# VectorE makes the low halves of two contexts before the masking passes of the same step, instead of after them

## What is computed

```python
def gnn(h, Wq, bq, Wk, bk, Wv, bv, Wf, bf, mask):
    q, k, v = heads(h @ Wq + bq), heads(h @ Wk + bk), heads(h @ Wv + bv)
    scores = einsum('bhqd,bhkd->bhqk', q, k) / sqrt(64)
    probs = softmax(scores + where(mask, 0, -9e15), axis=-1)
    ctx = einsum('bhqk,bhkd->bhqd', probs, v)
    return merge_heads(ctx) @ Wf + bf

for layer in (0, 1):
    h = maximum(layernorm(x), 0)
    x = x + gnn(h, *weights[layer], adj)
```

## Time and profile before

| | |
|---|---|
| median of three runs | 1950.31 us |
| profiled execution | 1948.68 us, span 1946.9 us |
| PE matmuls busy | 1838.3 us, 94% of the span |
| DVE busy | 1640.3 us, 84% |
| ACT busy | 1549.7 us, 80% |
| POOL busy | 1485.0 us, 76% |
| DMA | 61.5% of 16 engines, 187 GB/s |
| granted TensorE clock, mean | 0.997 |

### The profile page before, as it was taken

How to read it: one execution, slowest core, us unless ns; L and a number is a source line. 1 busy time by engine, 2 the same in 40 slices (tenths; PEclk the granted TensorE clock), 3 DMA queues, 4 the chain that set the end, 5 groups by cost and what they waited for, 6 DMA issues and landing times.

```text
span 1946.9 us, 54319 instructions
## 1 busy us (share of the span) xinstructions
PE 1838.3 (94%) x17210; PEld 1040.0 (53%) x17210; DVE 1640.3 (84%) x5555; ACT 1549.7 (80%) x4789; POOL 1485.0 (76%) x1777
## 2 busy tenths in 40 slices
PE   8899999999999999999999999999999999999998
PEld 3455555555555555555555555555555555555554
DVE  7988888888888888888888888888888888888876
ACT  5768878888887888788788888888887888788874
POOL 4568887887788788878878887887888788778762
PEclk8999999999999999999999999999999999999999
DMA  6556666666666666666666666666666666665555
GB/s 198 166 151 186 196 190 185 183 193 192 195 184 190 187 189 196 196 185 181 194 191 195 190 186 181 189 197 194 183 190 186 193 191 191 182 185 174 177 166 187
DMA packets 439942, 363.32 MB, mean 187 GB/s; under 512 B 207700, under 2 KB 406888, under 8 KB 439656
## 3 DMA queue, kind: packets, MB, share of 16 engines
q1 hardware_dynamic: 439656, 359.86, 61.5%
HBM read 184.30 MB, written 175.37 MB: 185 GB/s over the span
## 4 chain that ended last, share of the span: by engine, by line
PE 56%; DVE 33%; issue 7%; POOL 1%; DMA 1%; SPq 1%; ACT 1%; DVEq 0%; POOLq 0%; ACTq 0%
PE ps_shared L665 13%; PE ps_shared L667 12%; PE ps_shared L666 12%; DVE probs L1289 11%; PE ps_qk L665 6%; PE ps_qk L667 6%; PE ps_qk L666 6%; DVE p_blocks L1230 6%; DVE ct_lo L1263 6%; DVE h_blocks L1230 3%; DVE stats L1225 3%; DVE qk_lo L1269 1%; DVE x_tile L1300 1%; SPq L367 1%; DMA p_dram<-p_blocks 1%
## 5 line engine op out<-in xcount | busy, mean ns | idle before, releaser
L540 POOL TENSOR_TENSOR probs<-probs,row_rcp 128x768 f32<-128x768 f32 x252 | 371.3, 1473 | 308.9 <-DVE row_rcp L1254 308.9
L986 ACT ACTIVATE probs<-probs,row_min 128x128 f32<-128x128 f32 x1512 | 582.8, 390 | 2.5 <-DVE row_min L1289 2.5
L1289 DVE CUSTOM_DVE_ANT_0 probs<-ps_scores,mask,minus_scale 128x128 f32<-128x128 f32 x1512 | 430.9, 348 | 1.7 <-issue 1.2
L552 POOL TENSOR_TENSOR p_half<-p_moved,p_half 128x768 f16<-128x768 f32 x236 | 387.4, 1642 | 2.0 <-ACT p_half L961 2.0
L1300 DVE SCALAR_TENSOR_TENSOR x_tile<-ps_shared,out_scale,x_tile 128x384 f32<-128x384 f32 x256 | 157.9, 617 | 229.6 <-PE ps_shared L667 224.5
L948 ACT ACTIVATE v<-ps_shared 128x384 f16<-128x384 f32 x236 | 115.6, 490 | 262.2 <-PE ps_shared L667 262.2
L665 PE MATMUL ps_shared<-wv_hi,ht_hi 128*128 128x384 f16 x756 | 246.8, 326 | 81.4 <-DVE ct_lo L1263 81.4
L1269 DVE SCALAR_TENSOR_TENSOR qk_lo<-ps_qk,qk_bias,qk_hi 128x512 f16<-128x512 f32 x384 | 276.0, 745 | 39.8 <-ACT qk_hi L969 39.5
L986 ACT ACTIVATION_READ_ACCUMULATOR probs<-probs,row_min 128x1 f32 x1512 | 287.0, 190 | 0.0
L969 ACT ACTIVATE qk_hi<-ps_qk,qk_bias 128x512 f16<-128x512 f32 x384 | 257.6, 671 | 14.7 <-PE ps_qk L667 14.6
L536 POOL TENSOR_TENSOR x_tile<-x_tile,out_bias 128x384 f32<-128x384 f32 x256 | 257.5, 1007 | 1.1 <-DVE out_bias L1213 1.1
(11 more groups left out here) (144 smaller groups left out, 3967.3 us busy)
## 6 DMA issues: line engine op xcount, KB each, us to landing
p_dram<-p_blocks SPq DMA_DIRECT2D x256, 384.0 KB, 2.4
p_moved<-p_dram SPq DMA_DIRECT2D x1024, 96.0 KB, 2.4
h_dram<-h_blocks SPq DMA_DIRECT2D x252, 192.0 KB, 2.5
h_moved<-h_dram SPq DMA_DIRECT2D x1008, 48.0 KB, 2.0
x_tile<-in_x SPq DMA_DIRECT2D x128, 192.0 KB, 2.8
out_x<-x_tile SPq DMA_DIRECT2D x128, 192.0 KB, 2.5
adj_u<-in_adj SPq DMA_DIRECT2D x64, 64.0 KB, 2.5
wv_raw<-in_L_gnn_Wv SPq DMA_DIRECT2D x2, 576.0 KB, 4.7
```

What stands on the lines that cost most here:

```text
L540: nc.gpsimd.tensor_tensor(probs_of(t, i), probs_of(t, i), row_rcp[i % 2][:, :].rearrange("p (a o) -> p a o", o=1) .to_broadcast([P, HEADS, ...
L552: nc.gpsimd.tensor_tensor(p_part(i, 1), p_moved[i % 2][:, :, :].rearrange("p a n -> p (a n)"), p_part(i, 0), ALU.subtract).then_inc(p_set, 1)
L986: ins = nc.scalar.activation(tile[:, s, :], tile[:, s, :], ACT.Exp, bias=row_min[i % 2][:, s:s + 1], scale=-1.0, accum_out=row_sum[i % 2][ ...
L1289: ins = nc.vector.tensor_tensor_reduce(tile[:, s, :], score_bank(i, s // PAIRS)[:, (s % PAIRS) * P:(s % PAIRS + 1) * P], mask[b][:, i, :], ...
```

## The change

In `slot` of the DVE program, the calls of `ctx_lo` for the two contexts of an even step stand before `mask_and_min(t, i)` instead of after it. In odd steps there is no `ctx_lo`, so nothing moves there. No instruction is added or removed, and no other engine's list changes. The semaphore waits in `ctx_lo` (for `ct_hi_set`) and in `mask_and_min` (for `scored`, `mask_set`, `p_blocked`) go with their calls.

```diff
                     if exists(eu):
                         invert_sums(eu, ei)
-                    if exists(t):
-                        mask_and_min(t, i)
                     for cu, ci in pair_at(t, i):
                         if exists(cu):
                             ctx_lo(cu, ci)
+                    if exists(t):
+                        mask_and_min(t, i)
                     if t == 1:
                         weights_lo(1, CAST_ORDER[i])
```

## The result

The changed kernel takes 1856.04 us, the median of four runs (1854.17 to 1859.71), against 1949.99 us for the kernel before in the same job. The ratio is 0.952, with a 95% interval of 0.9504 to 0.9536. The forecast was 1852.3 us in a range of 1847 to 1868. In the profiled executions the span went from 1946.9 to 1852.4 us, 94.5 us less.

The account below looks back on a forecast made before the run. PE, nearly always busy, was taken to be held up by waits for DVE's ct_lo. Removing about 119 stalls, 98 us in all, from 1950.3 us gave 1852.3 us, range 1848 to 1859, widened to 1847 to 1868.

Parts of the forecast that it names:

- The bound: PE standing still for ct_lo of DVE before project_v in even steps: 83.8 us in 122 waits, some 0.8 us each.
- The move of the low halves: On DVE in even steps, ct_lo comes 1.63 us earlier, covering PE's stall with 0.84 or 0.80 us to spare.
- The masks 0.9 us later, and the wait in front of them: On DVE in even steps, masks end about 0.94 us later and stand behind ct_lo's wait for ct_hi: cost nothing.
- The sum: About 119 stalls lost 100 us: 96 us regular, 4 us from longer ones; 98 us taken as gain.
- DMA has no place on this path: On the path after the even-step stall goes, transfers were claimed to play no part; no size given.
- PE's busy time stays at 1838: Profile sign if right: PE's busy time unchanged at 1838 us, its share rising to about 99%.
- No change: Rival: DVE, not PE, sets the pace, so time stays at 1950 us; chance 0.03.
- The partial rival: Rival: DVE late by r beyond 0.45 us before the output, i = 2; r = 0.5 gives 1882 us; chance 0.08.
- The slower rival: Rival: late ct_hi makes DVE wait in front of the masks, delaying PE; up to 2065 us; chance 0.04.
- its decision point: Delay of the second ct_hi against DVE beyond which a pair of steps gets longer than before: 2.03 us.

Follow-up runs that it names:

- the shortened PE: PE leaves out two matmuls in each even step: 1952.71 us in the old order, 1830.44 us in the new order.
- the half change: The kernel before, with the low halves ahead of the masks only in even steps with i = 0: 1902.67 us.
- the runs with three and four passes ahead: Changed kernel with the two low halves behind the third or fourth of the six masking passes: 1858.54 us and 1886.08 us.
- the old order with the fifth DMA: Kernel before, with SP moving each h_moved by five DMAs instead of four, same bytes: 1955.11 us, ratio 1.0024.
- a shift of 1.76 us: Changed kernel with ACT making the two high halves behind p_hi, relu and h_hi instead of in front: 1944.26 us.
- a DVE that was 0.40 us later: Changed kernel with two unneeded statistics passes on DVE behind qk_lo_out in steps with i = 2: 1859.39 us.
- the run with the latest high halves: Changed kernel with ACT making the high halves behind the last qk_hi_out of the even step: 2093.94 us.
- the new order with the fifth DMA: Changed kernel with SP moving each h_moved by five DMAs instead of four, same bytes: 1938.04 us.

## Why the prediction was right

**The bound.** Right. The 83.8 us row was the pace: the shortened PE shows that PE's work did not count before, and the half change shows that each stall counts.

**The move of the low halves.** Right, to 0.02 us: the runs with three and four passes ahead find PE's cover at about 0.82 us, against 0.84 and 0.80 by the rows.

**The masks 0.9 us later, and the wait in front of them.** Right: no cost. `qk_lo` kept its time, DVE's wait for the output went from 224.5 to 122.1 us (forecast 127), and ACT's wait before `v_out` in the step shown is 0.65 us (forecast 0.64).

**The sum.** 94 us came instead of 98. The two traces, compared where each group of scores begins, say where the rest is. The changed kernel enters the slots 0.6 us later. The change is not the cause: scores that start at 68.78 us in the kernel before start at 69.41 in the changed one, and at 69.59 in the old order with the fifth DMA. Up to the scores at 101.65 in one and 102.30 in the other, removing two stalls gained nothing, as forecast, since DVE sets the pace there. Then PE waits longer for `qk_lo` than in the earlier trace rows:

```profile
102.30 0.29 PE L779 MATMUL ps_scores<-qk_hi 64*128 64x128 f16 x2 [2.67 <-DVE qk_lo L1269]
```

and the clock falls behind this gap. Another 0.5 us is lost by 118, although a third stall is gone there. From there to the tail the gain is 95.8 us, where I had written 98. The stalls in question were 118, not 119, and came to 97.4 us: the wait of 2.35 us in the tail, shown above, was counted among the 119 and cannot go by this change. The remaining 1.6 us are two pairs after the change that are 0.39 and 1.07 us too long. In the second of them ACT waited for `p_moved` and `h_moved`, DVE for `qk_hi`, and PE, before the scores, for `qk_lo`:

```profile
1342.67 0.23 PE L779 MATMUL ps_scores<-qk_hi 64*128 64x128 f16 x2 [1.00 <-DVE qk_lo L1269]
```

It began with one `p_dram` that took 4.75 us to land instead of the usual 2.4, so that SP could bring back `p_moved` only 4.82 us after its issue:

```profile
1322.69 0.38 SPq L360 DMA_DIRECT2D p_dram<-p_blocks  x1
...
1327.51 1.74 SPq L367 DMA_DIRECT2D p_moved<-p_dram  x4
```

SP's next step took 6.25 us (1331.25 to 1337.50), near its least, and its blocks still came late. The kernel before has landings of up to 4.46 us as well, but its ACT waited for such blocks only 9 times.

**What I had wrong.** The step that failed is "DMA has no place on this path". The forecast did not depend on it, but SP's list had only some 0.2 to 0.3 us a pair left after the change. This is an estimate: 14.02 − 13.75 = 0.27 from the shortened PE, and 0.90 − 0.73 = 0.17 from the fifth DMA, whose pairs take 14.76 us on the mean against 14.03. This is where the late pairs come from. "PE's busy time stays at 1838" was wrong too (1822.2): closing 121 stalls also hides the 0.16 us of record in front of each, by the prediction's own reading of the rows. The spread of the runs is wider than before (1854 to 1860 against 1949.5 to 1951); that late landings make this spread was not shown, only that they cost time in the profiled execution.

**The rivals.** "No change" by the busy share failed with the result: DVE at 84% was not the engine to relieve. The prediction read its page too narrowly there: in the Trainium skill, the page Perfetto Trace Analysis (section Identifying the Most-Contended Engine) wants TensorE judged by the matmul work done against its peak as well as by the weight-load share. From the counts and shapes of the matmuls in the trace and the peak on that page, the first is 88% before (an estimate), above DVE's 84%, so the page did not clearly speak for this rival. The partial rival's price was wrong as well: it asked r for each step from 0.45 us on, and a DVE that was 0.40 us later than that cost nothing in the typical pair. The slower rival's mechanism is real (high halves late enough make the kernel slower than before), and its decision point was roughly right: with a shift of 1.76 us a typical pair was 0.3 us shorter than in the old order, as 2.03 − 1.76 = 0.27 says. In the change itself it played no part, since `ct_hi` comes when it did.

## What to carry to other kernels

Read a stall by two numbers: how long the waiting engine stands, and what stands in the producer's queue between its last input and the piece that is waited for. If that piece's inputs are there earlier, put it ahead of work that nobody needs for longer than its own length; it need only be early enough: the run with three passes ahead gained all but 2.5 us of what the whole move gained. Then list every queue's remaining pause at the new pace, the DMA issuer's with the landings that it waits for included, since that is where the next bound comes from.

## What was unexpected of the hardware

The granted clock fell to its lower level (1.2 of 2.4 GHz, 0.50) in two short stretches of the start in which the kernel before stayed at 1.00. Its row is the first below, then two stretches of the changed kernel. The columns are the stretch, its length, the busy times of PE, PEld, DVE, ACT and POOL with counts, the granted clock, and DMA.

```profile
72.00:74.00 2.00, 1.61 (x8) 0.79 (x9) 1.97 (x6) 1.20 (x2) 1.83 (x4) 1.00 0.46 147
```

```profile
72.00:74.00 2.00, 1.74 (x11) 0.79 (x8) 1.80 (x3) 1.83 (x4) 1.94 (x3) 0.50 0.39 80
...
100.00:102.00 2.00, 0.00 (x0) 0.00 (x0) 2.00 (x3) 2.00 (x9) 2.00 (x1) 1.00 0.33 69
102.00:104.00 2.00, 1.70 (x34) 1.71 (x36) 2.00 (x4) 1.22 (x7) 1.12 (x2) 0.50 0.16 34
```

Ahead of the second, PE had stood for 2.67 us (1.42 in the kernel before, where the clock stayed up). All five other runs with a stall of 2.67 us or more at this place show the same fall. Ahead of the first, PE had stood for 2.38 us, but it had stood for 2.37 us in the kernel before too, and there the clock stayed up:

```profile
68.78 0.23 PE L779 MATMUL ps_scores<-qk_hi 64*128 64x128 f16 x2 [2.37 <-DVE qk_lo L1269]
```

The old order with the fifth DMA does show the fall at this place, so the first stretch is not an effect of the change: after stalls of 2.4 us both outcomes occur. Stalls of 1.66 us every 15.8 us, in the run with the latest high halves, left the clock at 1.00 from 160 to 1900 us. So the length of a stall alone does not tell the outcome. In the new order with the fifth DMA the clock did fall in the middle of the run; PE had stood for 2.25 us, until 1055.04, ahead of this row:

```profile
1056.00:1058.00 2.00, 2.00 (x40) 1.80 (x38) 1.97 (x5) 1.27 (x7) 0.86 (x1) 0.50 0.78 198
```

In the Trainium skill, the page TensorE: Matmul & The Clock Gate (section Part 1) says that the array's clock is passed at half rate when PE has not been busy recently; the rows agree, and they show that a start which is paced by another engine can lose twice.

SP's issue of a DMA mostly takes 0.35 to 0.5 us, and four mostly take 1.74. The landing of `p_dram` that SP waits for takes 2.4 us on the median and up to 4.75. One more issue in each step, with no byte more to move, cost 82 us where SP's list was full and 5 us where it was not.
